# The last feed-forward of a four-layer megakernel: every expert on every token, or 23 tiles of routed rows

## The reference

```python
logits = xt @ gate_w.T                      # xt: 1024 x 128, layer-normed
topk_w, topk_i = top_k(softmax(logits), 2)
combine = (one_hot(topk_i, 8) * topk_w[..., None]).sum(axis=1)
g, u = einsum('nd,edf->enf', xt, gate_k), einsum('nd,edf->enf', xt, up_k)   # f: 512
eo = einsum('enf,efd->end', silu(g) * u, down_k)
y = einsum('end,ne->nd', eo, combine)
shared = silu(xt @ sh_gate) * (xt @ sh_up) @ sh_down                        # width 256
x = x + tanh(g_ffn[3]) * (y + shared)
```

## Time and profile before

| what | us |
|---|---|
| median of 3 runs (824.75 to 832.76) | 824.98 |
| span of the profiled execution, first to last instruction | 818.0 |
| last stage, from the first matmul of expert 0 to the last addition | 650.3 to 815.6 |
| PE busy of 818.0 | 765.1 |
| DVE busy of 818.0 | 606.8 |
| ACT busy of 818.0 | 452.1 |
| POOL busy of 818.0 | 192.6 |

### The profile page before, as it was taken

One profiled execution on the slowest core, in us unless ns is written; L12 is line 12 of the kernel. 1 busy time (PEld: TensorE's weight loads), 2 busy tenths in 40 slices (PEclk: granted clock), 3 DMA queues, 4 the chain that ended last, 5 costly groups with the idle time before them and its releaser, 6 DMA issues. The chain is left out here.

```text
span 818.0 us, 14348 instructions
## 1 busy us (share of the span) xinstructions
PE 765.1 (94%) x5276; PEld 554.6 (68%) x5276; DVE 606.8 (74%) x1157; ACT 452.1 (55%) x681; POOL 192.6 (24%) x160
## 2 busy tenths in 40 slices
PE   5999889989999999999989988999998899999998
PEld 4655556756677687777776556666776777777776
DVE  6688676787676487888767887875655887878875
ACT  4477442256655507999825765566544255555553
POOL 3000100034635601223210002236446101111111
PEclk9999999999999989999999988999999999999999
DMA  9200000220230200000270000002311000000000
GB/s 346 85 2 2 1 0 1 99 108 2 53 79 2 52 1 2 1 0 1 103 328 2 1 2 1 2 2 52 80 27 27 1 1 1 0 1 0 0 1 27
DMA packets 3949, 30.56 MB, mean 37 GB/s; under 512 B 592, under 2 KB 944, under 8 KB 2352
## 3 DMA queue, kind: packets, MB, share of 16 engines
q1 hardware_dynamic: 3888, 29.73, 10.9%
HBM read 29.10 MB, written 0.62 MB: 36 GB/s over the span
## 5 line engine op out<-in xcount | busy, mean ns | idle before, releaser
L187 PE MATMUL banks<-normed_t_high,work_split 128*128 128x512 f32 x250 | 108.9, 435 | 4.9 <-DVE normed_t_low L325 2.6
L1135 POOL TENSOR_TENSOR work<-work 128x512 f32<-128x512 f32 x64 | 86.3, 1357 | 114.0 <-ACT work L1099 114.0
L744 DVE TENSOR_REDUCE work<-banks 128x2 f32<-128x512 f32 x128 | 84.5, 688 | 24.3 <-PE banks L459 17.8
L189 PE MATMUL banks<-normed_t_high,work_split 128*128 128x512 f32 x250 | 100.4, 402 | 0.0
L188 PE MATMUL banks<-normed_t_low,work_split 128*128 128x512 f32 x250 | 100.4, 402 | 0.0
L1945 ACT ACTIVATE work<-banks 128x512 f32<-128x512 f32 x68 | 40.7, 599 | 73.6 <-PE banks L189 73.6
L187 PE MATMUL banks<-work_split 128*128 128x512 f32 (+1 forms) x160 | 66.4, 415 | 4.8 <-DVE work_split L2023 3.3
L2056 DVE TENSOR_TENSOR work<-work,banks 128x512 f32<-128x512 f32 x68 | 46.7, 686 | 32.5 <-ACT work L1945 31.9
L952 PE MATMUL banks<-work 128*64 128x256 f32 x512 | 63.9, 388 | 2.6 <-ACT work L1099 2.2
L187 PEld LDWEIGHTS banks<-normed_t_high,work_split 128*128 128x128 f32 x250 | 47.7, 191 | 25.6 <-issue 12.6
L1787 DVE TENSOR_TENSOR work_split<-work,work_split 128x512 fp32r<-128x512 f32 x64 | 52.1, 815 | 16.8 <-ACT work_split L1709 16.3
(11 more groups left out here) (300 smaller groups left out, 1751.2 us busy)
## 6 DMA issues: line engine op xcount, KB each, us to landing
raw_b<-in_wf SPq DMA_DIRECT2D x1, 6528.0 KB, 19.2
raw_a<-in_wf SPq DMA_DIRECT2D x1, 4096.0 KB, 12.2
raw_b<-reciprocal_rows SPq DMA_DIRECT2D x6, 512.0 KB, 5.8
raw_a<-reciprocal_rows SPq DMA_DIRECT2D x6, 512.0 KB, 5.7
raw_a<-in_wf SPq DMA_DIRECT2D x1, 2048.0 KB, 14.3
raw_b<-in_wb SPq DMA_DIRECT2D x1, 2048.0 KB, 19.4
raw_a<-in_wb SPq DMA_DIRECT2D x1, 2048.0 KB, 8.6
small_operands<-in_small SPq DMA_DIRECT2D x1, 1386.0 KB, 10.2
```

Source lines behind the costliest of these rows:

```text
L187: nc.tensor.matmul(o, w[0], m[0], start=start, stop=False)
L189: return nc.tensor.matmul(o, w[1], m[0], start=False, stop=stop)
L744: nc.vector.tensor_reduce(a_nm[:, t:t + 2, j], bank(7 - n % 2).rearrange("p (e k) -> p e k", e=2), AX.X, ALU.max, negate=True).then_inc(A[ ...
L1135: nc.gpsimd.tensor_tensor(w_ps[g % 2].rearrange("p (h q) -> p h q", h=2), v[:, :, 0, :], v[:, :, 1, :], ALU.add).then_inc(W["ps"].sem, 1)
```

## The change

The 1024 x 2 pairs (token, choice) get slots, expert by expert, each expert's part rounded up to whole tiles of 128; 16 + 7 = 23 tiles hold every case, and all 23 are computed whatever the routing is. POOL writes the normed rows to their slots in HBM (16 indirect transfers of 128 rows, 130 columns of 4 bytes: the features, the row's number and its weight), SP loads the tiles back, and for each tile PE transposes the 128 tokens, multiplies with the tokens stationary and the tile's expert as the moving operand at an address held in a register, transposes the hidden part, and multiplies down. The weighted result goes to HBM by one indirect transfer a tile (23); rows of empty slots carry a number out of bounds and are dropped. SP reads both choices of every token back, and DVE adds them to the residual. The shared expert is computed between the router and the tiles.

All experts' high parts are made by ACT (4 and the shared one before the last layer norm's copies, 4 after the first shared Silus), all low parts by DVE, the shared one's by POOL, into one buffer over `raw_b`, `raw_a` and part of `work`. `f3_first` is gone from the attention's end, and so are two of POOL's clears. At the start SP fills the slots in HBM with empty rows (1.5 MB, behind all first loads), and before the last attention's spreads it loads the row numbers.

```diff
+W_ALL = E * W_F3 + W_SH
+TILES = 2 * NT + E - 1
+ROW = D + 2
+NO_ROW = 2 * T
...
+rows_t = sb("sublayer_out_t_and_context_tokens", [P, 2 * NT * ROW])
+out_t = rows_t[:, 0:T]
+ctok = rows_t[:, T:2 * T].rearrange("p (t d) -> p t d", t=NT)
+rows = rows_t[:, :].rearrange("p (c t d) -> p c t d", c=2, t=NT)
+both = nc.alloc_sbuf_tensor_at("expert_weights_low_and_high", [P, 2 * W_ALL], F32R, offset=split_at)[:, :]
...
+slot_rows = nc.dram_tensor("rows_by_slot", (TILES * P, ROW), F32, kind="Internal").ap()
+done_rows = nc.dram_tensor("rows_by_choice", (2 * T, D), F32, kind="Internal").ap()
+LOADS = (range(0, 4), range(4, 2 * NT), range(2 * NT, TILES))
...
+LOW_POOL, LOW_DVE = (E,), (0, 1, 2, 3, 4, 5, 6, 7)
+HIGH = (E, 0, 1, 2, 3, 4, 5, 6, 7)
+def f3_high_act(act, places):
+    if places[0] == 0:
+        act.wait_ge(ld["f3"], 16)
+        W["o"].wait(act, 1, 2 * NQ)
+    for n in places:
+        nc.scalar.activation(piece(w_high, HIGH[n]), piece(raw_b, HIGH[n]), ACT.Copy).then_inc(s_kh, 1)
...
+def f3_low(eng, e):
+    eng.wait_ge(s_kh, HIGH.index(e) + 1)
+    return eng.tensor_tensor(piece(w_low, e), piece(raw_b, e), piece(w_high, e).bitcast(F32), ALU.subtract)
+def f3_low_pool(pool):
+    for e in LOW_POOL:
+        f3_low(nc.gpsimd, e).then_inc(s_klp, 1)
+def f3_rows_pool(pool):
+    pool.wait_ge(ld["rows"], 32)
+    pool.wait_ge(s_row2, 1)
+    pool.wait_ge(s_slot, 1)
+    for c in range(2):
+        for t in range(NT):
+            at = c * NT + t
+            nc.gpsimd.indirect_dma_start(slot_rows, bass.IndirectOffsetOnAxis(slots_t[:, at:at + 1], 0),
+                                         rows[:, c, t, :], None).then_inc(s_put, 16)
+            pool.sem_inc(s_putn, 1)
+def f3_pool(pool):
+    for k in range(TILES):
+        pool.wait_ge(s_ky, k + 1)
+        nc.gpsimd.indirect_dma_start(done_rows, bass.IndirectOffsetOnAxis(tile_row(k)[:, D:D + 1].bitcast(U32), 0),
+                                     k_y[k % 3], None, bounds_check=NO_ROW - 1, oob_is_err=False)\
+            .then_inc(s_gone[k % 3], 16)
...
+    sp.wait_ge(s_put, 16 * 2 * NT)
+    for g, tiles in enumerate(LOADS):
+        n = len(tiles)
+        if tiles[0] < 2 * NT:
+            dst = rows_t[:, ROW * tiles[0]:ROW * (tiles[0] + n)]
+        else:
+            at = 4864 + ROW * (tiles[0] - 2 * NT)
+            dst = wf[:, at:at + ROW * n]
+        sp.dma_start(dst.rearrange("p (k r) -> p k r", k=n),
+                     slot_rows[P * tiles[0]:P * (tiles[0] + n), :].rearrange("(k p) r -> p k r", p=P))\
+            .then_inc(s_got[g], 16)
+    for k in range(3):
+        sp.wait_ge(s_gone[k], 16 * len(range(k, TILES, 3)))
+    for h in range(2):
+        sp.dma_start(k_back[h].rearrange("p (j d) -> p j d", j=NT),
+                     done_rows.rearrange("(p h j) d -> p h j d", h=2, j=NT)[:, h]).then_inc(s_all[h], 16)
...
+    pe.wait_ge(s_klp, 1)
...
+    def ranks():
+        two = chosen.rearrange("p t e -> p (t e)")
+        pe.wait_ge(ld["routing"], 16)
+        pe.wait_ge(s_two, 1)
+        nc.tensor.matmul(ps[:, 4, 0:(NT + 1) * E], k_before, two, start=True, stop=False)
+        for n in range(1, NT + 1):
+            last = nc.tensor.matmul(ps[:, 4, n * E:(NT + 1) * E], k_ones, two[:, 0:(NT + 1 - n) * E],
+                                    start=False, stop=n == NT)
+        last.then_inc(s_rank, 1)
...
+    for n in range(2 * NT):
+        pe.wait_ge(s_putn, n + 1)
+        stream(3, 4)
+    pe.wait_ge(s_off, 1)
+    offsets = [pe.value_load(k_offsets[0:1, k:k + 1], min_val=0, max_val=(E - 1) * W_F3) for k in range(TILES)]
...
+    def up(k):
+        if k >= TILES:
+            return
+        if k == 0:
+            pe.wait_ge(s_klp, len(LOW_POOL))
+            pe.wait_ge(s_kld, len(LOW_DVE))
+        if k % 4 == 0:
+            pe.wait_ge(s_gl, k // 4 + 1)
+        if k >= 2:
+            pe.wait_ge(s_ka, k - 1)
+        x = [v[:, (k % 4) * P:(k % 4 + 1) * P] for v in k_g[k // 4 % 2]]
+        for n in range(2):
+            w = [both[:, bass.ds(offsets[k] + (at + n * 512), 512)] for at in (W_ALL, 0)]
+            mm3(bank(2 * n + k % 2), x, w).then_inc((s_kg, s_ku)[n], 1)
+    def turn(k):
+        if k >= TILES:
+            return
+        pe.wait_ge(s_ka, k + 1)
+        if k >= 1:
+            pe.wait_ge(s_kal, k)
+        for f in range(NF):
+            last = nc.tensor.transpose(ps[:, 4, f * P:(f + 1) * P], k_af[k % 2][:, f * P:(f + 1) * P], ident)
+        last.then_inc(s_kt, 1)
+    def down(k):
+        pe.wait_ge(s_kal, k + 1)
+        if k >= 2:
+            pe.wait_ge(s_ky, k - 1)
+        hi, lo = k_a[k % 2]
+        for f in range(NF):
+            w = w_pair[:, :, bass.ds(offsets[k] + (1024 + f * P), P)]
+            nc.tensor.matmul(ps[:, 5 + k % 2, 0:2 * P].rearrange("p (s c) -> p s c", s=2), hi[:, f * P:(f + 1) * P], w,
+                             start=f == 0, stop=False)
+            last = nc.tensor.matmul(ps[:, 5 + k % 2, P:2 * P], lo[:, f * P:(f + 1) * P],
+                                    both[:, bass.ds(offsets[k] + (W_ALL + 1024 + f * P), P)],
+                                    start=False, stop=f == NF - 1)
+        last.then_inc(s_kd, 1)
+    group(0)
+    up(0)
+    up(1)
+    turn(0)
+    for k in range(TILES):
+        if k % 4 == 0 and k // 4 + 1 < len(GROUPS):
+            group(k // 4 + 1)
+        up(k + 2)
+        turn(k + 1)
+        down(k)
...
+    act.wait_ge(s_xn, NT * 8)
+    nc.scalar.activation(rows[:, 1, :, 0:D], rows[:, 0, :, 0:D], ACT.Copy).then_inc(s_row2, 1)
...
+    gated(0)
+    gated(1)
+    f3_high_act(act, range(5, 9))
...
+    for k in range(TILES):
+        if k % 4 == 0 and k // 4 + 1 < len(GROUPS):
+            group(k // 4 + 1)
+        silu(k + 2)
+        turned(k + 1)
+        half_down(k)
...
+    nc.vector.tensor_tensor(chosen[:, 0:NT, :], one, two, ALU.add).then_inc(s_two, 1)
+    past, chunk, where = rcol2[:, 0:E + 1], rbias, t1.rearrange("p t e -> p (t e)")[:, 0:2 * NT]
+    order.done(nc.vector.memset(past[:, 0:1], 0.0))
+    dve.wait_ge(ld["rows"], 32)
+    order.step(nc.vector.tensor_scalar(rows[:, :, :, D + 1], mcol2.rearrange("p (c t) -> p c t", c=2), gate[:, 7:8], None,
+                                       ALU.mult))
+    dve.wait_ge(s_rank, 1)
+    order.step(nc.vector.tensor_scalar(chunk, ps[:, 4, NT * E:(NT + 1) * E], 63.5, CEIL, ALU.add, ALU.add))
+    order.step(nc.vector.tensor_tensor_scan(past[:, 1:E + 1], chunk, col("less_ceil"), 0.0, ALU.add, ALU.add))
+    order.step(nc.vector.tensor_tensor(lg, ps[:, 4, 0:NT * E].rearrange("p (t e) -> p t e", t=NT),
+                                       past[:, 0:E].unsqueeze(1).to_broadcast((P, NT, E)), ALU.add))
+    order.step(nc.vector.tensor_tensor(ex2.rearrange("p (c t) e -> p c t e", c=2), pair,
+                                       lg.unsqueeze(1).to_broadcast((P, 2, NT, E)), ALU.mult))
+    order.step(nc.vector.tensor_reduce(where, ex2, AX.X, ALU.add))
+    nc.vector.tensor_copy(slots_t[:, :], where).then_inc(s_slot, 1)
+    order.step(nc.vector.tensor_tensor(k_past, k_starts.unsqueeze(2).to_broadcast((1, TILES, E - 1)),
+                                       past[0:1, 1:E].unsqueeze(1).to_broadcast((1, TILES, E - 1)), ALU.is_ge))
+    order.step(nc.vector.tensor_reduce(k_passed, k_past, AX.X, ALU.add))
+    nc.vector.tensor_scalar(k_offsets, k_passed, float(W_F3), None, ALU.mult).then_inc(s_off, 1)
...
+    for e in LOW_DVE:
+        f3_low(nc.vector, e).then_inc(s_kld, 1)
...
+    def weighted(k):
+        dve.wait_ge(s_ky2, k + 1)
+        if k >= 3:
+            dve.wait_ge(s_gone[k % 3], 16 * (k // 3))
+        nc.vector.scalar_tensor_tensor(out=k_y[k % 3], in0=ps[:, 5 + k % 2, P:2 * P], scalar=tile_row(k)[:, D + 1:D + 2],
+                                       in1=k_y2[k % 2], op0=ALU.mult, op1=ALU.add).then_inc(s_ky, 1)
...
+    dve.wait_ge(s_hb, 2)
+    for h in range(2):
+        dve.wait_ge(s_all[h], 16)
+        r = res[:, 4 * h:4 * h + 4, :].rearrange("p t d -> p (t d)")
+        for c in range(2):
+            ins = nc.vector.tensor_tensor(r, r, k_back[h][:, 512 * c:512 * (c + 1)], ALU.add)
+            if c:
+                ins.then_inc(s_res, 1)
...
+    load(slot_rows.rearrange("(k p) r -> p k r", p=P), empty_row.unsqueeze(1).to_broadcast((P, TILES, ROW)), "rows")
+    load(rows[:, :, :, D:ROW], row_ids, "rows")
+    f3_sync(sp)
+    f3_low_pool(pool)
+    f3_rows_pool(pool)
+    f3_high_act(act, range(0, 5))
+    wide_dve(dve, order, 1, raw_a, RB3, lambda: wide_first(1, 6, 7), lambda k: None)
-    wide_dve(dve, order, 1, raw_a, RB3, lambda: wide_first(1, 6, 7), lambda k: f3_first(dve, k))
-    pool.wait_ge(s_clear, 2)
+    norm_dve_tokens(dve, order, 7, res, rows[:, 0, :, 0:D], None, lambda h: wide_half(1, 6, h), 1)
```

More of the change, by code:

```diff
@@ L2065, in body @@
[L2065 to L2079 removed]
+            one, two = pair[:, 0], pair[:, 1]
+            pick_max(order, one, ex, t1, mcol2[:, 0:NT])
```

409 lines of the change are left out of this document (202 added, 207 removed).

## The result

The changed kernel takes 800.25 us (median of 4 runs, 797.56 to 801.44) against 826.32 for the kernel before in the same comparison (4 runs): ratio 0.967, 95% interval 0.962 to 0.972. It is faster by 26 us; I had forecast 35. The profiled execution took 801.44 us, its span is 799.6. The total came out inside the range. The times inside the last stage did not come out: two large errors of opposite sign met in the sum.

The account below looks back on a forecast made before the run. PE was taken to bound the kernel. Slots at 658, first tile at 688.0, clock 1.8, tiles 78.2 and pipeline 2.5 to 770.5, end 12.5: span 783.0, 35.0 less, so 825.0 - 35.0 = 790 us; range 770 to 817.

Parts of the forecast that it names:

- router's copy: Start of the last stage: DVE's copy of the router logits at 649.7 instead of 650.45, a gain counted as 0.8 us.
- slots to the first product of a tile: Lead-in of scatters, landing, load, address reads and transposes before the tiles; the gap from slots to first tile 28 to 32 us.
- first product to the last down: The tile loop on PE: 23 tiles at 3.4 us, 78.2 in all, plus 2.5 for filling and draining the pipeline.
- the end: After the tiles: last half-copy and sum, scatter, landing, reading back, four additions and the closing stretch, 12.5 us in all.
- p: Time of one indirect scatter on POOL, taken as 1.3 us between 0.5 and 3.6; 16 before the tiles make 20.8.
- about 685 if POOL stretches DVE: Before the tiles: end of DVE's low parts and additions if scatters stretch half of its 14.6 us of subtractions by 0.6.
- PE's shared products (5.6 + 5.4 us) and ACT's last four high parts lie inside: Between slots and tiles: this work was taken as hidden within the scatter and DVE branches, which tie at 684.
- The branch that I put at 680.5: DVE's work beside the scatters: addresses, products, low parts and two additions, 21.0 + 1.5 us after the slots at 658.
- PE's 23 addresses: Before the tiles: PE reads 23 offsets into registers at 0.3 us, 6.9 in all, of which 2.1 us show.
- Rival 1: Everything new is light: scatters under 1 us, address reads hidden, tile at 3.05, time 776; chance 0.18.
- Rival 2: Scatters slower but under a tile's time, 2.2 us each, 15.3 us more, time 805; chance 0.2.
- Rivals 3 and 4: PE's sequencer binding the tiles, 818 to 834, chance 0.12; POOL's scatters binding, 850 at 4.0 us each, chance 0.08.

Follow-up runs that it names:

- fixed addresses: Changed kernel with each tile's weights taken at a fixed address instead of one from a register, so other weights than the routing asks for: 801.81 us in one run.
- the reordered kernel: Kernel with register loads in the loop, plus the shared expert's chain reordered, low parts moved forward and 32 dummy products for 48: 787.95 us, ratio 0.956.
- the fastest: Kernel with register loads in the loop, plus shared low part on DVE, three experts' low parts moved forward and 28 dummy products without a wait: 778.9 us, ratio 0.945.

## Why the prediction was right in the sum and wrong in its terms

The span was to be 783.0 and is 799.6, 16.6 us more. By the steps of the prediction:

| step | forecast | measured | difference |
|---|---|---|---|
| router's copy | 649.7 | 657.16 | +7.5 |
| copy to slots | 8.3 | 9.9 | +1.6 |
| slots to the first product of a tile | 30.0 | 50.3 | +20.3 |
| first product to the last down | 82.5 | 70.0 | -12.5 |
| the end | 12.5 | 12.3 | -0.2 |

The start of the tiles is 29 us late and the tiles give 12.5 of it back. That the total came out is luck in part: with the start as forecast and these tiles the median would be about 771, with this start and the tiles as forecast about 813, both just inside a range of 47 us (770 to 817) that could not tell the two errors apart.

The forecast of the median is only 10 us low and not 16.6: 1.2 less because the median after lies 1.2 below the profiled execution, and 5.1 less because I added the 7.0 us between the median before and the span of its profile, where only 1.8 lie after. In every run on record with both, of either kernel and of the variants, the time is 1.8 to 3.0 us above the span. So the profiled execution before most likely took about 820 us and was a short one: its span of 818.0 is below, and its granted clock of 0.983 above, those of all 25 executions of that kernel that were timed beside the variants (819.6 to 829.6 us, 0.967 to 0.981). The spans of the two profiles differ by 18.4 us, the medians by 26.

By the time from the copy to the first product of a tile the lateness can be divided: 38.3 us were forecast and 60.2 measured, 21.9 more. Without dummy products and with the loads in the loop it is 44.6, so 15.6 of the 21.9 are these two together, and the 6.3 that are left are mostly DVE's branch behind the shared expert, whose last addition came 41.7 us after the copy.

**The late copy.** Of the 7.5 us, 0.8 is the gain that I had counted and that did not come; 1.6 the norm's products beside GpSimd (shown by moving GpSimd's part away); 0.8 the second eight logit products, 1.88 us at the lower level. The other 4.3 were there before the stage: DVE adds the second half of the attention's output at 645.86 instead of 641.54 (after, then before), and about 3 of these us fall at 303 to 318 us, where PE ran at the lower level.

```profile
645.86 0.69 DVE L1246 TENSOR_TENSOR normed_tokens<-normed_tokens,banks 128x512 f32<-128x512 f32 x1
```

```profile
641.54 0.69 DVE L1235 TENSOR_TENSOR normed_tokens<-normed_tokens,banks 128x512 f32<-128x512 f32 x1
```

Two programs alike up to there had either level, so this is a matter of the execution at least in part. Whether the change makes the lower level more frequent there, one profile of the kernel before, and that of a short execution, can't say; it stays open.

**Scatters: right in size.** p = 1.26 against 1.3. Sixteen took from 668.11 to 690.05, 21.9 us instead of 20.8. But "about 685 if POOL stretches DVE" looked at the wrong side: DVE's subtractions took 1.75 us beside the scatters and behind them alike, and the scatters became longer.

The inference that I quoted from the Trainium skill (SBUF — State Buffer, Who interferes with whom), that such subtractions would not slow descriptor generation, is contradicted for the scatter as a whole: pitch 1.26 alone, 1.66 to 2.27 beside them in the rows above. The scatter also reads its slot numbers from SBUF (`router_slots` in its row), and no run here tells the reading from the writing of descriptors.

**"PE's shared products (5.6 + 5.4 us) and ACT's last four high parts lie inside": the step that failed first.** I had counted these products' busy time and not their chain. Each down waits for an ACT step, two DVE steps and the up before it, and the clock was at the lower level, so the shared expert, 11.0 us of products in my count, began at 657 and ended at 688.6. With it went DVE's low parts (they ended at 697.6, and I had 679), which stand behind the hidden pieces in DVE's program. The branch that I put at 680.5 ended at 698.9, 41.7 us after the copy instead of 30.8.

**The dummy products were not in my sum.** I read the loop that issues three after every scatter as work beside the scatters. They are placed behind the shared downs in PE's program, and when PE is late they are a debt of 12.9 us; taking them out gave 11 to 13.

**PE's 23 addresses: the term was mis-sized.** 0.57 us each, where I took 0.3 between 0 and 1.7; and because the landing was long over, all 13.1 us showed and not 2.1.

The floor of about 600 ns that the Trainium skill (DMA: Bandwidth & Descriptors, Latency and other measured facts) gives for a `tensor_load` agrees with the 0.57 within 5%, if this read is that instruction.

**The tiles: cheaper than forecast.** 2.75 us, 2.84 with the groups, and not 3.4. A register in the address costs 0 (fixed addresses: 2.74), where I had 0.23; the 8% of handoffs is 0 (PE busy for 59.4 of 60.0 us in the loop), by my reading because PE's program runs two tiles ahead, which no run tests; and transposes take 0.35 instead of 0.5.

**Smaller slips in the working.** My own bounds (p to 1.7, tile to 3.6, reads to 0.6) add up to 808 and not 803. ACT's high parts were put at 1.5 us each where 1.15 us for 1024 columns gives 1.7; they took 1.4 and were hidden. And the nine slow products that I took the clock's 1.8 us from did not follow a long gap: PE had idled for 1.30 us at most in the 10 us before them.

**The rivals.** None of them happened. Rival 1 was nearest on the tiles (3.05 against 2.84) and missed the start by more than the forecast did. Rival 2 had 15 us of delay from p; the delay was there and p was not its cause. Rivals 3 and 4 are excluded: PE is full at clock 1.00 in the loop, and a scatter takes 0.98 of the 2.75 us. By my own test for the mechanism, "the gap between the slots and the first tile is not 28 to 32 us", I was wrong: it is 50.3.

## What to carry to other kernels

Follow a new side branch as a chain, engine by engine in program order, with each handoff, and not as a sum of busy times: what stands behind it in the same engine's program waits as long. Dummy work for the clock belongs into a wait that is sure to be there; in this case it is worth 2.6 us in the wait and costs 12.9 in front of the work. And when two branches end near each other, moving work from one into the other must be priced with what it does to the other engine: five of the eight low parts moved forward, with the chain reordered, left the first product where it was (43.9 us after the copy against 44.1), three brought it to 41.3.

## What the hardware did that I had not expected

- A load of an SBUF value into a PE register takes 0.57 us when 23 of them stand alone on PE, and 0.04 us of pace when each stands before its tile's first product in the loop.
- DVE's copies and subtractions on SBUF hold up GpSimd's issue of an indirect scatter: 0.96 us alone, 1.11 to 1.44 beside copies, 1.36 to 1.97 beside subtractions in the reordered kernel, and once 2.15 in the fastest. DVE's own time does not change: 1.75 us a subtraction of 1536 columns, beside scatters or alone.
- The other way round, GpSimd's subtraction of 768 columns more than doubled DVE's four one-input products beside it (1.12 to 2.68 us).
- The granted clock was at the lower of its levels (1.2 GHz) in the same stretch, 305 to 315 us, in ten of eleven profiles of the changed kernel and its variants, though PE was busy for 9.1 to 9.5 of these 10 us; two programs that are alike up to there had 0.50 and 0.92.
